# Attention batches written out without loops, and TensorE's projection or turn moved to the end of its step

## The reference: two layers of cross attention and mixture of experts

```python
# cross attention
q, k, v = heads(norm(x) @ Wq.T), heads(ctx @ Wk.T), heads(ctx @ Wv.T)
x = x + merge(softmax(where(mask, q @ k.T * SCALE, -1e9)) @ v) @ Wo.T
# the block with self-attention and experts
u = norm(x)
q, k, v = heads(u @ Wq + bq), heads(u @ Wk + bk), heads(u @ Wv + bv)
y = merge(softmax(q @ k.T / 4) @ v) @ Wo + bo
u = u + (norm(y) * ln1_g + ln1_b)
probs = softmax(u @ gate_w + gate_b)      # router; the experts' part follows, and x + all of it
```

## Time and profile before

| | us |
|---|---|
| median of three runs | 2591.42 |
| the profiled execution's own time | 2591.02 |
| its span, first to last instruction | 2589.3 |
| TensorE busy | 2222.8 |
| attention, first score of batch 0 to last score of batch 15 | 646.4 to 1857.8 |

### The profile page before, as it was taken

One profiled execution on the slowest core, in us unless ns is written; L12 is line 12 of the kernel. 1 busy time (PEld: TensorE's weight loads), 2 busy tenths in 40 slices (PEclk: granted clock), 3 DMA queues, 4 the chain that ended last, 5 costly groups with the idle time before them and its releaser, 6 DMA issues. The chain is left out here.

```text
span 2589.3 us, 37681 instructions
## 1 busy us (share of the span) xinstructions
PE 2222.8 (86%) x10760; PEld 1242.3 (48%) x10760; DVE 1304.4 (50%) x3466; ACT 1015.8 (39%) x1836; POOL 710.9 (27%) x718
## 2 busy tenths in 40 slices
PE   6878399984999898999999999999727999999990
PEld 2565266651333332334333333333326888888880
DVE  5556533313777576676777676677472111111115
ACT  2223112210555454555565555556502223233222
POOL 4114223323111001112123331323112334334335
PEclk9988699995999899999999999899958999999995
DMA  4327434427232232222234423234005666666664
GB/s 160 116 94 234 147 111 104 112 33 178 35 59 47 48 60 51 35 50 36 31 45 59 59 39 45 43 51 59 9 8 167 189 174 190 189 174 190 190 187 134
DMA packets 198682, 255.26 MB, mean 99 GB/s; under 512 B 21168, under 2 KB 176816, under 8 KB 196464
## 3 DMA queue, kind: packets, MB, share of 16 engines
q1 hardware_dynamic: 177968, 224.89, 34.1%
q0 software_dynamic: 20544, 28.33, 6.1%
HBM read 161.95 MB, written 52.67 MB: 83 GB/s over the span
## 5 line engine op out<-in xcount | busy, mean ns | idle before, releaser
L1782 ACT ACTIVATE att_prob<-att_ps 128x512 f32<-128x512 f32 x1024 | 599.5, 598 | 526.1 <-PE att_ps L1643 283.2
L1929 DVE CUSTOM_DVE_ANT_0 att_junk<-att_pm,bias 128x512 bf16<-128x512 f32 x512 | 344.2, 687 | 182.6 <-PE att_pm L1626 178.2
L1640 PE MATMUL att_ps<-att_qstack,att_kstack 99*128 99x512 bf16 x1024 | 397.7, 389 | 35.9 <-issue 26.2
L1925 DVE TENSOR_REDUCE att_tops<-att_pm 128x1 f32<-128x512 f32 x512 | 341.3, 684 | 159.0 <-PE att_pm L1626 154.0
L1626 PE MATMUL att_pm<-att_kstack,att_qstack 96*128 96x512 bf16 x1024 | 401.5, 393 | 12.2 <-DVE att_tops L1925 4.9
L1199 PE MATMUL exL_po<-exL_w,exL_hid 128*128 128x256 f32 x1696 | 379.4, 382 | 17.7 <-DVE exL_ys L1266 8.9
L1183 PE MATMUL exL_ph<-exL_xgT,exL_w 128*128 128x256 f32 (+2 forms) x1504 | 387.9, 413 | 5.7 <-ACT exL_hid L1216 3.0
L1216 ACT ACTIVATE exL_hid<-exL_ph,exL_b 128x256 f32<-128x256 f32 (+2 forms) x376 | 186.7, 501 | 439.4 <-PE exL_ph L1183 422.6
L1199 PEld LDWEIGHTS exL_po<-exL_w,exL_hid 128*128 128x128 f32 x1696 | 317.9, 190 | 70.7 <-issue 14.4
L1183 PEld LDWEIGHTS exL_ph<-exL_xgT,exL_w 128*128 128x128 f32 x1504 | 269.0, 191 | 109.9 <-issue 59.8
L1149 POOL DMA_INDIRECT sum<-exL_ys,exL_put x106 | 175.1, 1651 | 420.5 <-DVE exL_ys L1266 248.0
(11 more groups left out here) (310 smaller groups left out, 2403.2 us busy)
## 6 DMA issues: line engine op xcount, KB each, us to landing
exL_w<-in_L_W SPq DMA_DIRECT2D x94, 1024.0 KB, 5.1
att_qstack<-att_q SPq DMA_DIRECT2D x192, 128.0 KB, 5.9
kstack<-pick_k SPq DMA_DIRECT2D x48, 256.0 KB, 3.2
att_kstack<-kstack SPq DMA_DIRECT2D x16, 768.0 KB, 7.5
att_kstack<-att_k SPq DMA_DIRECT2D x96, 128.0 KB, 4.6
exL_b<-in_L_b SPq DMA_DIRECT2D x47, 128.0 KB, 5.3
values<-pick_vals SPq DMA_DIRECT2D x8, 574.0 KB, 4.5
att_vals<-values SPq DMA_DIRECT2D x8, 574.0 KB, 3.8
```

The costliest lines, as they stand in the source:

```text
L1640: mm = pe.matmul(ps[i % 2][:], stack["k"][par][0:KR + 3, h, kc * P:(kc + 1) * P], stack["q"][par][0:KR + 3, h, :], start=True, stop=me.self_)
L1782: act.activation(prob[i % PROBS][:], ps[i % 2][:], ACT.Exp, scale=SCALE).then_inc(s["p_ready"], 1)
L1925: ins = dve.tensor_reduce(tops[g % 2][:, t, j:j + 1], pm[i % TOPS][:], AX.X, ALU.max)
L1929: ins = dve.tensor_tensor_reduce(junk[:, i % TOPS, :], pm[i % TOPS][:], G["bias"][0][:, t, :], 1.0, -BIG / 2, ALU.add, ALU.max, tops[g % 2 ...
```

## The change

Two edits. `run` has two plain Python loops of eight batches in the place of the written-out batches and the `Fori` loops, so that all 16 batches are written out, all waits compare with constants and all chains have plain numbers. And in TensorE's `batch` the loop over the step's job pieces stands behind `score_step`, `max_step` and `value_quad`, where it stood ahead of them. ScalarE's, VectorE's, GpSimd's and SyncE's order within a batch is as it was. The bookkeeping for `chain.base` in the loops (GpSimd, VectorE) goes.

```diff
             before(Where(-1, False, None, False, start=True))
-            batch(Where(0, False, None, False), 0)
-            with eng.Fori(0, (B - 2) // 2) as pair:
-                batch(Where(pair * 2 + 1, False, False, False), 1)
-                batch(Where(pair * 2 + 2, False, False, False), 0)
-            batch(Where(B - 1, False, False, True), 1)
-            batch(Where(0, True, False, True), 0)
-            with eng.Fori(0, (B - 2) // 2) as pair:
-                batch(Where(pair * 2 + 1, True, True, True), 1)
-                batch(Where(pair * 2 + 2, True, True, True), 0)
-            last = Where(B - 1, True, True, None)
-            batch(last, 1)
+            for rows in range(B):
+                batch(Where(rows, False, False if rows else None, rows == B - 1), rows % 2)
+            for rows in range(B):
+                last = Where(rows, True, rows > 0, None if rows == B - 1 else True)
+                batch(last, rows % 2)
             behind(last.me, {bank: last.base(bank) + len(last.names(bank)) for bank in "ad"})
...
                     for g in range(NG):
                         for n in range(ROUND):
-                            for bank, name, piece in w.at(g * ROUND + n):
-                                if piece == 0 and name in ("att0-", "y0-"):
-
-                                    bank_, name_ = {"att0-": ("d", "out3-"), "y0-": ("a", "att1-")}[name]
-                                    pe.wait_ge(s["free_" + bank_], past(w.index(bank_, name_) + 1))
-                                if piece == 0 and name == "logits-":
-                                    pe.wait_ge(s["free_a"], past(w.index("a", "u1-") + 1))
-                                job(w.of(name), bank, name, w.index(bank, name), piece)
                             score_step(w.me, par, g, n)
                             if g < 2:
                                 max_step(w.me, par, g + 2, n)
...
                                     value_quad(w.me, par, g - 1, QUADS - 1)
                                 elif not w.first:
                                     value_quad(w.prev, 1 - par, NG - 1, QUADS - 1)
+                            for bank, name, piece in w.at(g * ROUND + n):
+                                if piece == 0 and name in ("att0-", "y0-"):
+
+                                    bank_, name_ = {"att0-": ("d", "out3-"), "y0-": ("a", "att1-")}[name]
+                                    pe.wait_ge(s["free_" + bank_], past(w.index(bank_, name_) + 1))
+                                if piece == 0 and name == "logits-":
+                                    pe.wait_ge(s["free_a"], past(w.index("a", "u1-") + 1))
+                                job(w.of(name), bank, name, w.index(bank, name), piece)
...
-                PPER = {False: 6 + 1, True: 12 + 1 + 2}
-                start = {}
-
                 def batch(w, par):
-                    rows, self_, _ = w.me
-                    if not isinstance(rows, int):
-                        chain.base, chain.n = (rows - 1) * PPER[self_] + start[self_], 0
-                    elif rows == B - 1:
-                        chain.base, chain.n = start[self_] + (B - 2) * PPER[self_], 0
                     if not w.last:
```

More of the change, by code:

```diff
@@ L1873, in batch @@
                         keep(w.next, 1 - par)
[L1874 to L1877, removed]
                 def behind(last, after):
@@ L2048, in before @@
                         cut_maxima(w.next, 1, 1, k)
-                VPER = {False: 5 * NG + 1, True: 4 * NG + 1 + 6}
-                start = {}
                 def batch(w, par):
[L2054 to L2058, removed]
                     for g in range(NG):
@@ L2088, in batch @@
                                 max_step(w.next, g - 2, n)
[L2089 to L2092, removed]
                 def behind(last, after):
```

## The result

The changed kernel takes 2519.68 us (median of four runs, 2516.47 to 2524.09) against 2591.89 us for the kernel before on the same chip (2586.67 to 2593.3). The ratio is 0.9726, 95% interval 0.9706 to 0.9747: 72 us faster. The profiled execution took 2520.9 us with a span of 2519.1.

A forecast was written before the change was run, and what follows sets the result against it. TensorE was taken as the bound. Jumps 25.8, cross batches 6.5, batches 0, 7, 8 and 15 1.1, 1.5, 1.9 and 0.7, batches 9 to 14 21.9: 59.4 us off 2591 gives 2532 us, range 2514 to 2558.

The forecast's parts named there:

- Jumps: Cross attention, batches 2 to 5: writing out the loops removes the back jumps, 12.97 and 12.82 us, together 25.8 us.
- Order in the cross attention: TensorE's jobs last in their step: waits of att0- and att1- go, 1.08 us a batch, 6.5 us in batches 1 to 6.
- perhaps 0.2 us a batch better: VectorE and GpSimd: dropped empty instructions and register work, counted as nothing because hidden behind TensorE, perhaps 0.2 us a batch.
- Self attention: Batches 9 to 14: jobs last saves 0.44 + 0.7 + 0.84 = 2.0 us each; the group gains 21.9 us.
- That start can't move: Self attention: turn0+ follows VectorE's last xn piece, believed without idle time, so removing two job waits gains only 0.44 us.
- What is saved behind step 32 is given back: Ends of self-attention batches: savings after step 32 only lengthen the wait for negated maxima, from 1.5 to about 2.8 us.
- The clock: Ends of batches 9 to 14: longer waits bring half-clock spells; six of 1.0 us allowed, bounds 0 and 6 times 2.4.
- the rival: Ends of batches 9 to 14: half clock costs 6 x 2.4 us instead of 6, giving 2540 us; chance 13 in 100.
- The order is worth nothing: Whole attention: only the loops count, 25.8 us plus about 8 in self attention, giving 2557 us; chance 10 in 100.
- Slower by ScalarE's copy: Copies delay exponentials and scores, 0.5 us for each of some 136 kind a jobs, 68 us: 2625 us; chance 4 in 100.
- late fetch: Batch boundaries: written-out code fetched too late, 10.5 us each, six needed to undo the gain; chance 3 in 100.
- More than forecast: Attention: no half clock, no spells at logits-, shorter VectorE chain ahead of turn0+, giving 2518 us; chance 8 in 100.

The follow-up runs named there:

- the short loops: Changed kernel plus a three-pass loop over one empty instruction on TensorE at the start of batches 1 to 6: 2523.53 us, ratio 0.9734.
- the early cut: Changed kernel with GpSimd's second cut moved ahead of add_y and its SyncE fill ahead of group 3's negated maxima: 2505.15 us, ratio 0.9671.

## Why the prediction was right

The mechanism held in the main, and the sum came out 11 us short: 59.4 us forecast, 70.1 between the two profiled executions. About 5 us of that are a term sized too small, 4.5 us lie outside the part that was changed, and the rest is spread over the cross attention.

- Jumps, 25.8 us: measured 25.8. That it is no bare branch was argued against the branch times in the Trainium skill's "Advanced Engine Details and Errata", section "Control Flow Timing"; the short loops (0.0 us) and the 6.2 to 10.6 us of the long ones agree. The wait itself was thought of as one thing, and is two: refetch and contention.
- Order in the cross attention, 1.08 us a batch: 1.07 and 1.12 (batches 1 and 6 with the order alone). The register work "perhaps 0.2 us a batch better": 72.45 against 72.63, so 0.2.
- Batch 7: 1.5 forecast, 1.9 measured. Batch 8: 1.9 and 1.8. Batch 0: 1.1 and 1.3. Batch 15: 0.7 and 0.8.
- Self attention, 2.0 us a batch at full clock: 3.0 in batch 9 (75.36 to 72.39). This is the term that was mis-sized, and the step that failed in it is "That start can't move". VectorE's last piece of `xn` started 11.02 us into batch 9 before, 10.85 with the order alone, 10.79 with the writing-out alone and 10.61 with both, and `turn0+` went from 11.61 to 11.15: its chain carried register work and empty instructions, with stops of 0.10 us that are 0.03 without the loops, and one of 0.09 us ahead of a maximum that is gone with the order. The prediction gave it no idle time. By S33 the batch is 2.4 us earlier with the order alone and 2.6 with both, where 2.0 was forecast. And the stretch from `add_y` to the next first score, taken as fixed, is 26.5 us with loops and 26.2 without. (The prediction's "the same 26.5 us hold in batches 9 to 11" is a misreading: they are 26.5 in 9, 13 and 14, but 28.8 in 10, which ends in a jump, and 29.4 and 31.0 in 11 and 12, where 10.2 us of it are at half clock.) Six batches make 5.2 us of the 11.
- "What is saved behind step 32 is given back": right. The wait grew to 2.89 us (2.8 forecast), and was 2.7 to 2.9 us at four of six ends. That the end hangs on the second cut and its fill is shown by the early cut, which removes it.
- The clock: six spells of 1.0 us allowed; batches 9 to 14 took 440.5 us, 6.2 more than six times 72.39, hence 1.0 each. Five of the six spells stand at the ends of batches, these two stretches at the first:

```profile
1365.00:1368.40 3.40, 3.40 (x13) 0.75 (x13) 2.24 (x7) 1.68 (x5) 0.00 (x0) 0.50 0.00 0
1368.40:1372.00 3.60, 3.60 (x23) 1.49 (x22) 3.53 (x14) 2.38 (x5) 1.26 (x2) 1.00 0.01 2
```

They begin 0.9 us behind the first score of batch 10 that waited 2.89 us: half clock for 3.4 us, full clock behind it. The spell of batch 11 lasts 6.8 us and begins in the wait itself; batch 14 has one of 3.4 us at its start and the sixth, of 3.4 us, behind `logits-`. They take 74.28 and 73.85 us. So the warning of the Trainium skill ("TensorE: Matmul & The Clock Gate", "HAM oscillation — how this bites in real kernels") is borne out in kind: an idle stretch of 1.9 to 2.9 us at a turn of a batch lowered the clock five times out of five (the one of 1.27 us did not), at a price of 1.0 us and not the 2.4 of the rival.

4.5 us of the gain lie ahead of the attention, whose first score comes at 641.8 us instead of 646.4. Nothing there was changed; in the seven other kernels it came between 641.7 and 645.4. This stays unexplained and was not forecast.

The rivals. "The order is worth nothing" fell with 25 us for the order alone. "Slower by ScalarE's copy" has a true core: scores wait for exponentials 21 times, 5.8 us in total, where the kernel before had this line, so its price was 3.3 us and not 68; a value quad or a job nearly always stood between, as argued.

```profile
PE att_ps L1640 <- ACT att_prob L1782: 2.5, 6, 0.6
```

No boundary showed a late fetch. "More than forecast" (2518 us) had the nearest number and part of the reason: VectorE's chain ahead of `turn0+` got shorter and the spells behind `logits-` became fewer and shorter, but half clocks did occur. That the total landed 2 us from it is partly luck, as 4.5 us of the gain lie where nothing was changed.

## What to carry to other kernels

Read a loop's jump from whole turns, not from its idle time alone, and ask two things: how long the body is, and what the DMA engines carry at that moment; a bulk load can be moved off the jump, a long body can be written out. An order of work that shortens one engine's batch shows its worth only if what ends the batch (here one cut and fill on GpSimd and SyncE) is moved as well, and that chain, once seen in the profile, was worth another 14 to 18 us by moving two calls. When two edits are tried apart, their gains need not add: here the jumps of the self attention held TensorE longer when it came to them earlier.

## What the hardware showed that was not expected

- A jump back over two batches of code: 10.1 to 10.6 us of idle TensorE with a load of 1.5 MB issued at the same time, 6.2 to 6.5 without it, 1.2 to 6.9 in the self attention, the longest where SyncE's fills still ran 1.8 to 2.2 us into the wait; short loops on TensorE in six batches: 0.0 us. Why 6.3 us remain on almost empty DMA engines, for fetches of 0.3 to 2.2 us each that follow one another with pauses, is open.
- Straight code of 16 batches was never late: 65 fetches of 16 KB and 64 of 8 KB in the whole run, and no wait without a releaser in the attention.
- Writing the batches out saved TensorE 0.42 us of 73.7 even in a batch with no jump, most of it in waits for VectorE, which is busy 72% of a cross batch: an engine with slack still sets the start of single jobs. Empty instructions and register-compared waits on VectorE are the likely cause.
- In batches 9 to 14 of all the kernels, spells at half clock begin at two places only: at waits of 1.5 us or more between two batches, and 0.7 to 3.5 us behind the start of the router's small matmuls. Where those wait 0.7 to 0.8 us first, the spells last 6.8 or 10.2 us; where they don't, 3.4 us.
